# Vision tower kernel, first stage: token tiles of 112, swapped queries by ScalarE copies, ScalarE normalisation, keys' high half last

## The reference, cut to what matters

```python
h = einsum('bnp,dp->bnd', patches, W) + b             # 768 -> 256
m, v = mean(h), var(h); xn = (h - m) / sqrt(v + eps)  # over the 256
Q, K, V = xn @ Wq, xn @ Wk, xn @ Wv                   # 16 heads of 16
term2 = einsum('bhqd,kd->bhqk', Q, r); term4 = einsum('hd,kd->hk', v, r)
scores = (Q.K + u.K + rel_shift(term2 + term4)) / 4   # r: sines and cosines of a distance
```

## Time and profile before

| | us |
|---|---|
| median of 3 runs | 3623.16 (3621.20 to 3627.92) |
| the profiled execution | 3636.08 |
| its span in the trace | 3634.4 |
| first stage: first embedding matmul | 24.28 |
| first stage: last work on GpSimd ends, about | 663.5 |

### The profile page before, as it was taken

One profiled execution on the slowest core, in us unless ns is written; L12 is line 12 of the kernel. 1 busy time (PEld: TensorE's weight loads), 2 busy tenths in 40 slices (PEclk: granted clock), 3 DMA queues, 4 the chain that ended last, 5 costly groups with the idle time before them and its releaser, 6 DMA issues. The chain is left out here.

```text
span 3634.4 us, 89293 instructions
## 1 busy us (share of the span) xinstructions
PE 3229.9 (89%) x34825; PEld 2526.0 (70%) x34881; DVE 2623.7 (72%) x6129; ACT 1498.6 (41%) x2991; POOL 1617.8 (45%) x1965
## 2 busy tenths in 40 slices
PE   6999999399999999999996722999599999998997
PEld 6888887378888888888883311778377777775876
DVE  5888888568888888888884676554266666665887
ACT  3444444056666666666663310332133333332221
POOL 2555555256666666666662010577200000004776
PEclk9999999579999999999998855999799999998999
DMA  4666665736556565665654611354333333225776
GB/s 141 185 185 197 195 186 161 189 84 164 157 149 172 136 166 148 160 162 148 170 133 131 182 30 34 110 140 126 95 116 111 107 104 106 95 90 135 217 219 165
DMA packets 449244, 518.11 MB, mean 143 GB/s; under 512 B 64150, under 2 KB 418804, under 8 KB 448397
## 3 DMA queue, kind: packets, MB, share of 16 engines
q1 hardware_dynamic: 427376, 473.19, 46.1%
q0 software_dynamic: 21504, 39.94, 4.1%
HBM read 306.93 MB, written 215.94 MB: 144 GB/s over the span
## 5 line engine op out<-in xcount | busy, mean ns | idle before, releaser
L1281 POOL DMA_INDIRECT sb_ye<-scratch_ye,sb_table x224 | 240.8, 1075 | 805.6 <-DMA sb_gw<-scratch_gw 733.3
L854 DVE TENSOR_REDUCE p_mx<-p_psS 98x2 f32<-98x390 f32 (+1 forms) x1024 | 527.1, 556 | 0.0
L800 ACT ACTIVATE p_after<-p_psF 98x392 f32<-98x392 f32 x512 | 255.1, 498 | 480.6 <-PE p_psF L946 472.5
L803 ACT ACTIVATE p_probs<-p_psE 98x392 f32<-98x392 f32 x1024 | 450.1, 496 | 0.0
L848 DVE COPY_PREDICATED p_psS<-p_later,p_psD 98x196 f32<-98x196 uint32 x1024 | 330.6, 362 | 120.0 <-PE p_psS L932 111.4
L749 POOL TENSOR_SCALAR_AFFINE_SELECT p_after<-p_after 98x392 f32<-98x392 f32 x512 | 274.4, 536 | 243.2 <-ACT p_after L800 243.0
L1269 POOL DMA_INDIRECT scratch_xe<-sa_xs,sa_table x224 | 222.2, 992 | 205.6 <-DMA sa_xs<-scratch_xf 140.4
L753 POOL TENSOR_SCALAR_AFFINE_SELECT p_probs<-p_probs 98x392 f32<-98x392 f32 x512 | 274.5, 536 | 85.8 <-ACT p_probs L803 80.2
L969 PE MATMUL p_psO<-p_probs,p_v 98*32 98x196 f32 x4096 | 279.8, 345 | 2.0 <-POOL p_probs L753 1.7
L419 POOL TENSOR_TENSOR p_rt<-p_rt 128x784 f32<-128x784 f32 x64 | 187.1, 2924 | 122.7 <-DVE p_st L397 122.7
L103 PE MATMUL p_psH<-p_wh,p_xh 128*98 128x256 bf16 x768 | 211.5, 275 | 24.3 <-DVE p_xl L334 24.3
(11 more groups left out here) (300 smaller groups left out, 10110.7 us busy)
## 6 DMA issues: line engine op xcount, KB each, us to landing
scratch_stack<-p_st SPq DMA_DIRECT2D x64, 784.0 KB, 6.0
p_x<-in_x SPq DMA_DIRECT2D x32, 1176.0 KB, 9.5
p_L<-scratch_stack SPq DMA_DIRECT2D x192, 196.0 KB, 4.3
p_U<-scratch_stack SPq DMA_DIRECT2D x192, 196.0 KB, 4.4
scratch_xe<-p_zero SPq DMA_DIRECT2D x32, 1024.0 KB, 5.9
ex_xin<-scratch_xe SPq DMA_DIRECT2D x56, 512.0 KB, 4.0
scratch_ye<-ex_y SPq DMA_DIRECT2D x56, 512.0 KB
scratch_h<-p_h SPq DMA_DIRECT2D x32, 392.0 KB
```

The source lines that it names most:

```text
L800: act.activation(after[c][:].rearrange("p h t -> p (h t)"), psF[:, 0:4 * TILE], ACT.Exp, scale=DK ** -0.5).then_inc(p_ok.sem, 1)
L803: act.activation(probs[c][:, b, :], psE[:, b, 0:PAIR], ACT.Exp, scale=DK ** -0.5).then_inc(p_ok.sem, 1)
L854: nc.vector.tensor_reduce(mx[g1][:, c, 4 * q1 + 2 * b:4 * q1 + 2 * b + 2], own, AX.X, ALU.max).then_inc(s_max.sem, 1)
L1281: nc.gpsimd.indirect_dma_start(out=ye[v][u][:, t, k, :], out_offset=None, in_=d["ye"], in_offset=bass.IndirectOffsetOnAxis(ap=table[:, at ...
```

## The change

Position u = 0 now embeds, normalises and projects to values 448 tokens as 4 tiles of 112 (WIDE), position u = 1 336 tokens as 3 tiles: over two positions 7 tiles stand in place of 8, and the transposed tokens nh, nl hold 784 columns from which keys and queries take their 392. The swapped queries are no longer a product: ScalarE copies the 64 upper partitions of a query tile in PSUM to the 64 lower ones of an SBUF tile qsw, and the lower to the upper. xn is made by ScalarE (Identity with a scale and a bias for each token); VectorE makes the bias, -mean/std (nmr), in its place. The keys' high half is made last in ScalarE's order, from k32 in SBUF. On VectorE the moments of n + 1 come ahead of xl of n + 2. On GpSimd both sums come ahead of both low halves. At the start the token weights and the first pixels are transferred first and split first. The diff, cut (waits that only guard the new buffers, and tile shapes, are left out):

```diff
--- before.py
+++ after.py
+WIDE = 112
+        def count(u):
+            return 4 - u
+        def tokens(u):
+            return WIDE * count(u)
...
-        nh, nl = sb("nh", [128, 2, PAIR], BF16), sb("nl", [128, 2, PAIR], BF16)
+        nh, nl = sb("nh", [128, 2, 2 * PAIR], BF16), sb("nl", [128, 2, 2 * PAIR], BF16)
+        new = [slice(0, tokens(0)), slice(tokens(0), 2 * PAIR)]
+        own = [slice(u * PAIR, (u + 1) * PAIR) for u in range(2)]
+        qsw = sb("qsw", [128, 2, PAIR])
...
+                sp.dma_start(w32[:], d["tok_w"]).then_inc(w_in, 16)
+                load(0, 0)
...
             def _(act):
...
-                act.wait_ge(loaded, 112)
-                act.activation(wh[:], w32[:], ACT.Copy).then_inc(w_hi, 1)
...
+                def normalise(n, u):
+                    act.wait_ge(rstd_ok.sem, rstd_ok.at(n))
+                    act.wait_ge(t_ok.sem, t_ok.at(n - 1))
+                    for t in range(count(u)):
+                        last = act.activation(xn[:, t, :], h0[u][:, t, :], ACT.Identity, bias=nmr[:, t:t + 1], scale=rstd[:, t:t + 1])
+                    last.then_inc(xn_ok.sem, 1)
...
-                        act.activation(nh[:], psT[:, :, 0:PAIR], ACT.Copy).then_inc(nh_ok.sem, 1)
+                        act.activation(nh[:, :, new[u]], psT[:, :, 0:tokens(u)], ACT.Copy).then_inc(nh_ok.sem, 1)
                     if known(n, 0, PAIRS - 2):
                         split(n + 2, u)
-                    def halves(m):
...
+                    if known(n, 1, PAIRS + 1):
+                        for m in range(2):
                             act.wait_ge(ab_ok.sem, ab_ok.at(n - 1, m + 1))
                             act.activation(st[1 - u][:, m, AH:BH + 1:2, :], rt[:, m, 0:4:2, :], ACT.Copy).then_inc(abh_ok.sem, 1)
...
-                    halves(0)
+                    if known(n, 0, PAIRS - 1):
+                        deviation(n + 1, 1 - u)
+                        normalise(n + 1, 1 - u)
...
-                    halves(1)
-                    if known(n, 0, PAIRS):
                         act.wait_ge(jk_ok.sem, jk_ok.at(n))
-                        act.wait_ge(st_out.sems[u], st_out.at(n - 2, u))
-                        act.activation(st[u][:, :, KH, :], psJ[0][:, :, 0:PAIR], ACT.Copy).then_inc(kh_ok.sem, 1)
-                    if known(n, 0, PAIRS - 1):
-                        deviation(n + 1)
...
                         act.activation(k32[:, :, 0:PAIR], psJ[0][:, :, 0:PAIR], ACT.Copy).then_inc(k32_ok.sem, 1)
...
                             act.wait_ge(jq_ok.sem, jq_ok.at(n, m + 1))
-                            act.activation(st[u][:, m, QH, :], psJ[(m + 1) % 2][:, 0, 0:PAIR], ACT.Identity,
+                            act.activation(st[u][:, m, QH, :], psJ[1][:, m, 0:PAIR], ACT.Identity,
                                            bias=cols[:, m, 0:1]).then_inc(qh_ok.sem, 1)
+                            act.wait_ge(rt_ok.sem, rt_ok.at(n - 1, m + 1))
+                            act.activation(qsw[0:64, m, :], psJ[1][64:128, m, 0:PAIR], ACT.Copy)
+                            act.activation(qsw[64:128, m, :], psJ[1][0:64, m, 0:PAIR], ACT.Copy).then_inc(qsw_ok.sem, 1)
+                        act.wait_ge(k32_ok.sem, k32_ok.at(n))
+                        act.activation(st[u][:, :, KH, :], k32[:, :, 0:PAIR], ACT.Copy).then_inc(kh_ok.sem, 1)
...
             def _(dve):
...
                     dve.wait_ge(std_ok.sem, std_ok.at(n))
-                    nc.vector.reciprocal(rstd[:], std[:]).then_inc(rstd_ok.sem, 1)
...
-                    for t in range(4):
-                        last = nc.vector.tensor_scalar(xn[:, t, :], h0[u][:, t, :], mv[:, t, 0:1], rstd[:, t:t + 1],
-                                                       ALU.subtract, ALU.mult)
-                    last.then_inc(xn_ok.sem, 1)
+                    nc.vector.reciprocal(rstd[:, 0:count(u)], std[:, 0:count(u)]).then_inc(recip_ok.sem, 1)
+                    dve.wait_ge(recip_ok.sem, recip_ok.at(n))
+                    nc.vector.scalar_tensor_tensor(nmr[:, 0:count(u)], mv[:, 0:count(u), 0], -1.0, rstd[:, 0:count(u)],
+                                                   ALU.mult, ALU.mult).then_inc(rstd_ok.sem, 1)
...
+                    if known(n, 0, PAIRS - 1):
+                        moments(n + 1, 1 - u)
                     if known(n, 0, PAIRS - 2):
                         split(n + 2, u)
-                    if known(n, 0, PAIRS - 1):
-                        normalise(n + 1, 1 - u)
...
-                        dve.wait_ge(jq_ok.sem, jq_ok.at(n, m + 1))
+                        q, swapped = psJ[1][:, m, 0:PAIR], qsw[:, m, :]
+                        dve.wait_ge(qsw_ok.sem, qsw_ok.at(n, m + 1))
...
-                        term(1, qb, 2)
-                        term(3, qb, 2)
-                        dve.wait_ge(qh_ok.sem, qh_ok.at(n, m + 1))
...
+                        term(0, q, 1)
+                        term(2, q, 1)
...
+                        term(1, swapped, 2)
+                        term(3, swapped, 2).then_inc(rt_ok.sem, 1)
...
                     for m in range(2):
-                        pool.wait_ge(q_used.sem, q_used.at(n, m + 1))
+                        pool.wait_ge(rt_ok.sem, rt_ok.at(n, m + 1))
                         nc.gpsimd.tensor_tensor(rt[:, m, 0:4:2, :], rt[:, m, 0:4:2, :], rt[:, m, 1:4:2, :], ALU.add).then_inc(ab_ok.sem, 1)
+                    for m in range(2):
                         pool.wait_ge(abh_ok.sem, abh_ok.at(n, m + 1))
...
             def _(pe):
...
-                    for t in range(4):
-                        cut = slice(t * TILE, (t + 1) * TILE)
+                    for t in range(count(u)):
+                        cut = slice(t * WIDE, (t + 1) * WIDE)
...
                         pe.wait_ge(v_ok.sem, v_ok.at(n))
                         for m in range(2):
-                            if m:
-                                pe.wait_ge(k32_ok.sem, k32_ok.at(n))
-                            ps = psJ[(m + 1) % 2]
-                            rows(ps[:, 0, 0:PAIR], 128 * m)
-                            rows(ps[:, 1, 0:PAIR], C + 128 * m).then_inc(jq_ok.sem, 1)
+                            rows(psJ[1][:, m, 0:PAIR], 128 * m, u).then_inc(jq_ok.sem, 1)
```

More of the change, by code:

```diff
@@ L256, in _ @@
             def _(act):
-                for s in (xh_ok, std_ok, nh_ok, k32_ok, kh_ok, qh_ok, abh_ok, v_ok):
+                for s in (xh_ok, std_ok, xn_ok, nh_ok, k32_ok, kh_ok, qh_ok, qsw_ok, abh_ok, v_ok):
                     s.open(act)
-                act.wait_ge(loaded, 112)
-                act.activation(wh[:], w32[:], ACT.Copy).then_inc(w_hi, 1)
-                for c in range(2):
-                    act.activation(by_dim(gh, c), by_head(g32, c), ACT.Copy).then_inc(w_hi, 1)
-                act.activation(gh[:, :, 3 * C:], g32[:, :, 3 * C:], ACT.Copy).then_inc(w_hi, 1)
                 def split(n, u):
@@ L345, in normalise @@
                     dve.wait_ge(stats_ok.sem, stats_ok.at(n))
-                    dve.wait_ge(std_ok.sem, std_ok.at(n - 1))
                     dve.sem_inc(passed, 1)
-                    for t in range(4):
+                    for t in range(count(u)):
                         last = nc.vector.bn_aggr(mv[:, t, :], stats[:, t, :])
@@ L431, in _ @@
                     s.open(pe)
[L432 removed]
+                pe.wait_ge(w_lo, 1)
                 pe.wait_ge(pads_set, 1)
@@ L443, in embed, with rows @@
                     last.then_inc(h_ok.sem, 1)
-                def rows(out, col):
+                def rows(out, col, u):
                     return three_products(nc, out, [
-                        (gh[:, c, col:col + 128], gl[:, c, col:col + 128], nh[:, c, :], nl[:, c, :]) for c in range(2)])
+                        (gh[:, c, col:col + 128], gl[:, c, col:col + 128], nh[:, c, own[u]], nl[:, c, own[u]]) for c in range(2)])
                 def position(n, u):
```

134 lines of the change are left out of this document (71 added, 63 removed).

## The result

The changed kernel takes 3642.93 us (median of 5 runs, 3641.3 to 3655.84), the kernel before, run beside it, 3624.67 (5 runs, 3621.2 to 3629.04). The ratio is 1.0059, 95% interval 1.0038 to 1.0080: slower by 18 us, where 3583 and a gain of 40 were forecast, and outside the range of 3537 to 3626. The profiled execution took 3641.3 us, 5.2 more than that of before.

The account below looks back on a forecast made before the run. PE was taken to bound the stage at 18.97 us a position, then a DVE, POOL, ACT and PE loop of 17.9: 1.07 x 31 = 33 us plus 7 at the start, 40 off 3623.2, so 3583, range 3537 to 3626.

Parts of the forecast that it names:

- What bounds: In the first stage PE is full at 18.97 us a position; after the change a loop through DVE, POOL, ACT and PE bounds.
- clock still 1.00: Sign to look for in a window of the stage: PE busy about 86% with its granted clock still full.
- The start: Before the first position: pixels arrive and are split earlier, first matmul at 16 us, gain 7 us, bounds 3 and 9.
- The keys' low half on POOL comes in between: In rotate, m = 0: POOL holds DVE out of the two swapped-query terms for 1.67 us; bounds nothing and 3.4.
- Reciprocal and nmr, 0.21 each: On DVE after the square root: two small operations of 0.21 us each, bringing the loop to 12.7 us.
- Normalisation on ACT: On ACT after nmr: 0.40 to 0.50 us a tile, taken as 0.45, 3.5 tiles, bringing the loop to 14.4 us.
- high half and two copies: On ACT after the queries, DVE waiting: 0.49 + 0.39 + 0.49 us, bringing the loop to 17.9 us.
- The clock falls: Rival: PE's pauses of about 1 us halve its clock, some 28 us a position, 290 us more; chance 0.03.
- The end of the stage stays as it is: At the end of the first stage: the change was taken to leave its time as before.
- POOL gets in twice: Rival: POOL's first sum also blocks rotate's m = 1 terms, loop 19.9 us, 22 us slower, 3645; chance 0.12.

Follow-up runs that it names:

- e1: The changed kernel with ScalarE making the keys' high half right after the f32 keys, ahead of the queries, instead of last: 3602.37 us, ratio 0.9927 to before.
- e3: The changed kernel with sixteen idle matmuls in PE's wait for nl at u = 0 positions, their output overwritten: 3612.82 us, ratio 0.9947 to before.
- e5: The changed kernel with the edits of e1 and e3 together: 3576.6 us, ratio 0.9856 to before.
- e2: The changed kernel with nmr made tile by tile, with rstd as a scalar operand: 3644.8 us, ratio 1.0047 to before.
- e6: The changed kernel with the normalisation back on VectorE, without nmr, the keys' high half still last: 3621.72 us, ratio 0.9981 to before.
- e9: The changed kernel with the edits of e7 and ten idle matmuls in PE's wait for nl: 3566.96 us, ratio 0.9822 to before.
- e10: The changed kernel with nl made between rotate's halves, PE's keys right behind it and ScalarE's key copies ahead of the square root: 3621.2 us, ratio 0.9973.
- e7: The changed kernel with the edits of e1 and e6 together: 3590.49 us, ratio 0.9883 to before.

## Why the prediction was wrong

**What bounds.** Right: the loop through DVE, POOL, ACT and PE took the bound from PE, and most of PE's 3.4 us did not arrive. But "clock still 1.00" failed, and with it the sum. That PE is busy 85.6% in the window, as forecast (86%), is luck: both the position and PE's matmuls, at half clock in part, were longer than in the forecast.

**The start.** Right: 7 us forecast, 6.9 to 7.3 measured (first matmul at 16.98 against 16.1).

**"The keys' low half on POOL comes in between".** Right in place and size: the high half is done at 309.99, POOL begins at 310.06, DVE loses 1.4 us against 1.7, and e1 shows that without it the kernel is faster than before; net of the copy that then stands ahead of the queries it costs 1.0 us (e3 against e5). m = 1 then starts at 4.63 us and rotate ends at 7.86 (8.1 forecast). The Trainium skill, SBUF — State Buffer, section Who interferes with whom, gives a shared port pair as an exclusive lock for which VectorE, with two SBUF inputs, and GpSimd block each other; the trace agrees (2.57 us against 1.15).

**"Reciprocal and nmr, 0.21 each".** Mis-sized: nmr took 1.06 at three tiles, and 0.63 at four, where one with POOL idle took 0.16, since it too takes two SBUF tensors while POOL runs. I let the rule hold for large operations and forgot it for one of three or four columns. On its own it changed nothing (e2), as PE's clock held V back as long.

**"Normalisation on ACT", "high half and two copies".** Too cheap: a tile starts 0.50 after the last (0.45), at the upper bound of the forecast. The high half and the two copies take 327.04 - 325.40 = 1.64 us instead of 1.37, since the next starts 0.61 after the high half (0.49) and 0.51 after the first copy (0.39): no overlap of 0.1 appears between them. Undoing the normalisation's move is worth 0.77 us a position with the clock falling (e6) and 0.64 with it full (e9 against e5); three tiles take 1.06 us on VectorE when POOL is idle, 1.58 on ScalarE: the rule of the Trainium skill, ScalarE: Activation LUTs, section Rules for kernel authors, to multiply and add on VectorE, which the prediction quoted against the change, held here.

**"The clock falls", chance 0.03: the step that failed.** The prediction saw pauses of "about 1 us" and no fall. It worked on the mean of both kinds of position. At a u = 0 position the embedding (54 matmuls, behind eight transposes) is over some 6 us after rotate begins, while nl comes at 9.0 by my own sum: a pause of 3 us, which was in the numbers and was averaged away. All 13 such pauses between 100 and 600 us were followed by half clock. That is what e3 shows to cost 0.76 us a position, half of the 1.5 us between 19.39 and 17.9. Nor did I price the fall between nothing and a whole stage at half clock (290 us): it came in stretches of 3.4 or 6.8 us. And the pauses "of 6 us and more" that I set against it are of 6.3 and 4.7 us in the trace of before.

**The other half of the 1.5 us is in the terms of the two entries before the clock**, nmr and what ScalarE does. It shows at a position whose clock stayed full, from the rotate at 327.04 to the one at 345.87: the normalisation begins 13.2 us in (12.7 forecast), the copy of V at 15.1 (14.3), the high half of the queries at 17.2 (16.45), the next rotate at 18.8 (17.9). It has half a tile more to normalise than the mean of the forecast, 0.25 us, and half a tile less of V to copy. So the clock alone does not make up the 46 us between 33 won and 13 lost in the 31 positions: with it held (18.63 us, e3) they would have won some 10 us, and the change would have been a small gain in place of a small loss, as e3 is (0.9947).

**"The end of the stage stays as it is."** Wrong by 5.1 us. From the last h0 to the first rotate after it are 12.5 us (9.8 before), from there to the last rotate 20.2 (18.95), from there to the memset 25.7 (24.6). PE's clock in windows of 20 us from 630 to 670 us is 0.76 and 0.67, where from 620 to 660 us before it was 0.90 and 0.76. No run tried this stretch by itself.

**The rival that gave nearly the right number** (POOL gets in twice, 3645) was right for the wrong reason. The first sum starts at 312.30 and the terms of m = 1 at 314.28 take 1.15 us; there is no second collision of rotate. Its other half, normalisations at 0.50, was seen.

What stays open: what exactly makes the clock fall. Of the pauses between 100 and 600 us, these had half clock within 3 us of their end: all 23 of 3.0 us and more (the change, e10), 14 of 14 of 1.76 us in e7, 7 of 14 of 1.88 in e1, 11 of 14 of 1.0 in e3, but only 3 of 13 of 1.0 in the change, and none of 14 of 1.68 in e5 and of 1.18 in e9. So the length of the pause alone does not decide below 3 us, and no run varied it by itself. And 7 of the 18 us of the medians are in no stage that the traces point to.

## What to carry to other kernels

When a change takes work off the bounding TensorE, follow each kind of iteration by itself and ask how long TensorE will now idle: the pause does not show in the mean of the loop, and the half clock behind it can cost more than a small gain is worth, if it falls on matmuls for which another engine waits. When a step is put last in an engine's order, look up who takes its result, and what that engine then runs against: here the place of one copy of 0.86 us was worth some 40 us by the medians, clock included. Apply the rule that VectorE and GpSimd exclude each other to small operations too, and do not trust it to stop at two SBUF inputs (below); and where two delays run in parallel, removing one alone shows nothing.

## What the runs showed of the hardware

- Sixteen matmuls that compute nothing made the kernel 30 us faster; with ten in e9 the granted clock went from 0.93 to 1.00 and a position from 17.72 to 16.97 us.
- Pauses of 3.0 us of TensorE were each followed by 3.4 or 6.8 us at the 1.2 GHz level; shorter ones were in one order of the work (all 14 of 1.76 us in e7, 11 of 14 of 1.0 us in e3) and not in another (none of 14 of 1.68 us in e5).
- Half clock cost 0.9 to 1.4 us (3.4 us of it) or some 2.5 (6.8 us) where ScalarE waited for the values, and nothing that shows at the u = 1 positions of the change and of e3, where it did not (18.83 us with and without).
- A VectorE operation on three columns with two SBUF inputs took 1.06 us while POOL ran; on four columns with POOL idle, at 31.39 us, 0.16. In the form with a scalar operand three of them took 0.46 us.
- A normalisation on VectorE reads only one tensor from SBUF, beside its scalars, and was still held by POOL: 1.77 us for three tiles in e6, where POOL's low halves ran beside it, 1.06 in e9, where they had ended. Two SBUF tensors, the condition of the prediction, are thus not the whole of it.
- Copies of 392 columns from PSUM on 64 partitions took 0.49 us each and started 0.51 us apart.
